# Four graph layers on one core: the attention scores of the edges looked up with a stationary table, edge scores made beside a dense layer, and fewer rows kept in DRAM

## The reference

```python
def gat_block(x, edge_index, edge_attr, ...):     # 3 heads, edge_attr is (E, 16)
    ...
    alpha = a_src[row2] + a_dst[col2] + a_edge    # per edge and head
    alpha = where(alpha >= 0, alpha, 0.2 * alpha)
    ex = exp(alpha - segment_max(alpha, col2)[col2])
    attn = ex / segment_sum(ex, col2)[col2]
    agg = segment_sum(attn[:, :, None] * xp[row2], col2)
```

## Time and profile before

| | |
|---|---|
| median of 3 runs | 3326.29 us (3325.86 to 3333.78) |
| the profiled execution | 3322.32 us, of which the span is 3320.7 us |
| PE busy | 2399.7 us, 72% of the span |
| DVE busy | 1563.3 us, 47% |
| POOL busy | 1430.9 us, 43% |
| ACT busy | 704.2 us, 21% |
| moved by DMA | 627 MB, 189 GB/s over the span |

### The profile page before, as it was taken

One profiled execution on the slowest core, in us unless ns is written; L12 is line 12 of the kernel. 1 busy time (PEld: TensorE's weight loads), 2 busy tenths in 40 slices (PEclk: granted clock), 3 DMA queues, 4 the chain that ended last, 5 costly groups with the idle time before them and its releaser, 6 DMA issues. The chain is left out here.

```text
span 3320.7 us, 68789 instructions
## 1 busy us (share of the span) xinstructions
PE 2399.7 (72%) x21724; PEld 2076.2 (63%) x21725; DVE 1563.3 (47%) x3763; ACT 704.2 (21%) x1093; POOL 1430.9 (43%) x1498
## 2 busy tenths in 40 slices
PE   1599999989899962999969992666530103999965
PEld 0466666679688841888859882566530103999954
DVE  5476666623311165111133335888879201555567
ACT  0077777726200042000010000000000100000033
POOL 4322222213200012122224446777778777776765
PEclk9899999989899975999989996777775555555577
DMA  4378888942688815888869995999972534655611
GB/s 129 99 226 275 275 279 283 285 146 70 182 284 282 282 46 170 252 248 250 249 196 296 290 292 137 184 186 189 182 170 76 160 106 117 153 142 145 144 37 43
DMA packets 560771, 627.36 MB, mean 189 GB/s; under 512 B 265887, under 2 KB 412524, under 8 KB 560041
## 3 DMA queue, kind: packets, MB, share of 16 engines
q1 hardware_dynamic: 258425, 387.60, 38.1%
q10 hardware_dynamic: 252072, 164.25, 19.6%
q0 software_dynamic: 50208, 74.70, 9.3%
HBM read 484.61 MB, written 142.11 MB: 189 GB/s over the span
## 5 line engine op out<-in xcount | busy, mean ns | idle before, releaser
L896 POOL DMA_INDIRECT rows<-x_rows,src_i x832 | 854.1, 1027 | 279.5 <-issue 236.1
L1570 PE MATMUL ps<-slices,wide 128*128 128x250 f16 x7350 | 829.0, 271 | 41.9 <-DMA slices<-adjacency 36.0
L1570 PEld LDWEIGHTS ps<-slices,wide 128*128 128x128 f16 x7350 | 715.9, 98 | 130.6 <-issue 24.2
L1802 PE MATMUL ps<-slices 128*128 128x75 bf16 x4992 | 248.2, 227 | 160.4 <-DVE slices L2544 160.4
L1802 PEld LDWEIGHTS ps<-slices 128*128 128x128 bf16 x4992 | 241.7, 118 | 166.9 <-issue 166.9
L936 POOL TENSOR_TENSOR ea_one<-ea,ones 128x64 f32<-128x64 f32 x250 | 133.9, 536 | 464.0 <-DMA ea<-in_edge_attr 447.0
L1510 PE MATMUL ps<-weighted,slices 128*128 128x57 f32 x1120 | 253.1, 417 | 69.5 <-DVE weighted L2124 69.5
L1510 PEld LDWEIGHTS ps<-weighted,slices 128*128 128x128 f32 x1120 | 247.1, 333 | 69.8 <-DVE weighted L2124 69.8
L1456 PE MATMUL ps<-rows,weighted 128*32 128x128 f32 x2000 | 274.5, 282 | 15.4 <-DMA ea<-in_edge_attr 13.4
L1510 PE MATMUL ps<-weighted,rows 128*128 128x57 f32 x544 | 130.6, 418 | 194.2 <-DMA rows<-x_rows,src_i 170.8
L1510 PEld LDWEIGHTS ps<-weighted,rows 128*128 128x128 f32 x544 | 123.4, 332 | 197.1 <-issue 171.0
(11 more groups left out here) (356 smaller groups left out, 3421.4 us busy)
## 6 DMA issues: line engine op xcount, KB each, us to landing
slices<-adjacency SPq DMA_DIRECT2D x525, 437.5 KB, 5.5
rows<-in_edge_attr SPq DMA_DIRECT2D x250, 256.0 KB
adjacency<-wide ACTq DMA_DIRECT2D x91, 437.5 KB, 3.1
adjacency<-slices ACTq DMA_DIRECT2D x84, 437.5 KB, 3.1
x_of_edges<-rows SPq DMA_DIRECT2D x140, 256.0 KB
slices<-x_of_edges ACTq DMA_DIRECT2D x140, 256.0 KB
slices<-src_low ACTq DMA_DIRECT2D x52, 512.0 KB
rows<-x_rows,src_i POOLq DMA_INDIRECT x832
```

What stands on the lines that cost most here:

```text
L896: pool.indirect_dma_start(out=packed[i][:, c, :], out_offset=None, in_=table, in_offset=bass.IndirectOffsetOnAxis(ap=rows_of, axis=0)).the ...
L1570: mm = pe.matmul(ps_d[b], high_low[:, part, QS * s + q, :], slices[:, s, PN * q:PN * (q + 1)], start=(s == 0 and q == 0 and part == 0), st ...
L1802: mm = pe.matmul(ps_g[:, s, b, c, 0:HEADS * QH], lowT[:, s, b, h, P * c:P * (c + 1)], tab_b[:, n, h, :, :].rearrange("p h i -> p (h i)"), ...
```

## The change

The lookup is turned round. The table (scaled by a power of two, as two fp16 numbers for each score: 17 high parts x 3 heads x 2 = 102 columns, in three parts of 128 sources) is now the stationary operand, and the comparison matrix moves, 512 edges at a time. The sources' low parts (now source modulo 384) are no longer broadcast by DMA: a 1 x 2048 row is loaded, PE spreads it over 128 partitions with a row of ones, and ACT copies the result out of PSUM. The high parts come as bytes, broadcast by DMA to 102 partitions. DVE picks by one comparison and product, and PE adds the picked rows. The scores go out head by head, ACT issues three small stores for each pass. POOL's wait for `scores_begun` is gone.

The edge scores leave this stage. They are made in the second dense product: SP loads the attributes of 32 edges of each partition for a block (`load_ea`), ahead of the last two slices, and DVE multiplies and reduces them (`edge_scores`) between `mean` and the copy of `yb`.

108 groups are stored in place of 140, and 100 are fresh; `sums` begins with 8 stored groups and then takes stored and fresh ones in turn. Some constants and the list of low and high parts are made by a few more small operations near the start and between the first and the second dense product.

```diff
-    KT = 2
-    QH = 25
+    KT = 3
+    QH = 17
+    HI_DIV = KT * P
+    QR = 2 * HEADS * QH
...
-    FRESH = 68
+    MIXED = NP
+    FRESH = RING * MIXED
     STORED = NG - FRESH
-    MIX = 3 * RING
+    FIRST = 2 * RING
+    MIX = 2 * RING
+    ESC = 32
...
+            def load_ea(c, i):
+                to = rows[:, 1 + i, :, :].rearrange("p c f -> p (c f)")[:, 0:ESC * EF].rearrange("p (j e) -> p j e", e=EF)
+                last = (P - 1) * EPP
+                sp.dma_start(to[0:P - 1, :, :], ea16[0:last, :].rearrange("(p j) e -> p j e", j=EPP)[:, bass.ds(ESC * c, ESC), :]
+                             ).then_inc(es_in[i], 16)
...
+                sp.dma_start(to[P - 1:P, 0:n, :], ea16[bass.ds(at, n), :].unsqueeze(0)).then_inc(es_in[i], 16)
...
                     for s in range(SL):
+                        if k == 1 and s == SL - 2:
+                            if not first:
+                                sp.wait_ge(es_made, 2 * q - 3)
+                            load_ea(q, b)
...
-                if SCORES_LEAD <= g < SCORES_LEAD + PASSES:
-                    pool.wait_ge(scores_begun, g - SCORES_LEAD + 1)
...
+            def store_as(k, s, first=False):
...
+                act.activation(as_o[:, s, :], ps_o[s], ACT.Copy).then_inc(as_copied, 1)
+                act.wait_ge(as_copied, u + 1)
+                for h in range(HEADS):
+                    act.dma_start(as_d[h:h + 1, bass.ds(SB * u, SB)].rearrange("h (j e) -> (h j) e", e=SQ), as_o[4 * h:4 * (h + 1), s, :]
...
+            def next_scores(k, s, first=False, begun=False, last=False):
+                u = 2 * k + s
+                copy_low(u + 2, s, 0)
...
+                    store_as(k - 1 + s, 1 - s, first=begun)
+                copy_low(u + 2, s, 1)
+                if not last:
+                    load_low(u + 4, s)
+                act.wait_ge(picked_ready, 2 * u + 2)
+                load_hi(u + 2, s)
...
+            def score_rows(u, s, b, first):
...
+                for h in range(KT):
+                    for c in range(2):
+                        mm = pe.matmul(ps_g[:, b, SQ * c:SQ * (c + 1)], tab_b[:, h, :, :, :].rearrange("p n h i -> p (n h i)"),
+                                       lowT[:, s, h, SH * b + SQ * c:SH * b + SQ * (c + 1)], start=(h == 0), stop=(h == KT - 1))
...
+            def edge_scores(c, u, i):
+                ea_c = rows[:, 1 + i, :, :].rearrange("p c f -> p (c f)")[:, 0:ESC * EF].rearrange("p (j e) -> p j e", e=EF)
+                v.wait_ge(es_in[i], 32 * (u + 1))
...
+                v.tensor_tensor(es_prod, ea_c.unsqueeze(1).to_broadcast([P, HEADS, ESC, EF]),
+                                we_b[:, :, :].unsqueeze(2).to_broadcast([P, HEADS, ESC, EF]), ALU.mult).then_inc(es_made, 1)
+                v.wait_ge(es_made, 2 * c + 1)
+                v.tensor_reduce(es[:, :, bass.ds(ESC * c, ESC)], es_prod, AX.X, ALU.add).then_inc(es_made, 1)
...
-                    lows(16 * (k + 1 + s), 1 - s)
...
+                    lows(u + 1, 1 - s)
+                v.wait_ge(hi_in[s], 16 * (k + 1))
...
+                    v.scalar_tensor_tensor(picked[:, b, :], hi_b[:, s, SH * b:SH * (b + 1)], seg_i[0:QR, 0:1], ps_g[:, b, :],
+                                           ALU.is_equal, ALU.mult).then_inc(picked_ready, 1)
```

More of the change, by code:

```diff
@@ L774, in body @@
                     sp.dma_start(xb[:, b:b + 1, :, :], tiles_of(rows_of, q)).then_inc(pair_landed[b], 16)
-                pairs(sp, body)
+                if k == 1:
+                    whole = (E - (P - 1) * EPP) // ESC // 2 * 2
+                    for q in range(2):
+                        body(q, 0, q, True)
+                    with sp.Fori(1, whole // 2) as u:
+                        for b in range(2):
+                            body(2 * u + b, u, b, False)
+                    for q in range(whole, NP):
+                        body(q, q // 2, q % 2, False)
+                    sp.wait_ge(es_made, 2 * NP - 3)
+                    load_ea(NP, NP % 2)
+                else:
+                    pairs(sp, body)
             load_rows_twice(d0, t["x"])
@@ new lines, in _ @@
+            for s in range(2):
+                next_scores(0, s, first=True)
+            next_scores(1, 0, begun=True)
+            next_scores(1, 1)
+            with act.Fori(2, NIT // 2 - 2) as k:
+                for s in range(2):
+                    next_scores(k, s)
+            for s in range(2):
+                next_scores(NIT // 2 - 2, s, last=True)
+            store_as(NIT // 2 - 2, 1)
+            for s in range(2):
+                store_as(NIT // 2 - 1, s)
+            for s in range(2):
+                act.wait_ge(as_stored[s], 16 * HEADS * (NIT // 2))
@@ L1810, in _, with score_pass @@
+            def score_pass(k, s, first=False, last=False):
+                u = 2 * k + s
+                score_rows(u, s, 0, first)
+                if not (first and s == 0):
+                    sum_picks(u - 1, 1 - s, 1, first)
+                if not last:
+                    spread_low(k + 1, s, 0)
+                score_rows(u, s, 1, first)
+                sum_picks(u, s, 0, first)
+                if not last:
+                    spread_low(k + 1, s, 1)
             scan_turns(0, *SCANS[0])
+            pe.wait_ge(scan_dve, 3)
@@ L1811, in _ @@
+            for s in range(2):
+                for b in range(2):
+                    spread_low(0, s, b, first=True)
             pe.wait_ge(prep_dve, MAX_DVE + 3)
-            with pe.Fori(0, NIT // 2) as k:
+            for s in range(2):
+                score_pass(0, s, first=True)
+            with pe.Fori(1, NIT // 2 - 1) as k:
                 for s in range(2):
-                    for b in range(2):
-                        score_rows(k, s, b)
+                    score_pass(k, s)
+            for s in range(2):
+                score_pass(NIT // 2 - 1, s, last=True)
@@ L1816, in _ @@
+            sum_picks(NIT - 1, 1, 1, False)
             for k in (1, 2):
@@ L2303, in layer0 @@
                 layer_norm(d0, s, n + 1, rb, yb, d0.done)
[L2305 removed]
+            part = [sums_b[:, n * HEADS * P:(n + 1) * HEADS * P] for n in range(2)]
             def weights_beside(q, s):
```

394 lines of the change are left out of this document (210 added, 184 removed).

## The result

| | before | after |
|---|---|---|
| median of four runs each | 3327.26 us | 3468.69 us (3464.78 to 3469.28) |
| ratio to before, 95% interval | 1 | 1.0426 (1.0408 to 1.0443) |
| span of the profiled execution | 3320.7 us | 3463.2 us |

The kernel became 4.3% slower. The stages of after, as in the earlier trace rows: length, busy PE, PEld, DVE, ACT, POOL, then PEclk, DMA share, GB/s. The first is the whole second dense product, the second a piece of the score stage, the third a piece of `sums`.

What follows compares the result with a forecast made beforehand. It took PE to bound the second dense product and POOL's gathers with PE's sums the last third; 3322.3 + 211 - 25 = 3508 us, hence 3512 because the median lies 4 us above the profiled run; range 3420 to 3610.

Steps and rivals of the forecast that it cites:

- The dense product: Second dense product: the 127-row load on one DMA engine sets a block's period, 22.6 us for 14.16, +211 us.
- the bounds: Second dense product: one DMA engine's rate lies between 18.9 and 28 GB/s, giving +304 to +91 us.
- Rival B: Second dense product: the 127 rows spread over many engines, or that engine has room; only -25 us left, 3301 us; chance 0.08.
- the signs I had named: Second dense product: 560 to 580 us, PE under 70% busy awaiting slices, under 245 GB/s, blocks of 20 to 26 us.
- D: Second dense product: PE idles some 8 us per block and runs the rest at 1.2 GHz; +354, 3655 us; chance 0.06.
- DVE's operations, the lists, the constants: Dense product and before: two DVE operations, 1.75 us each, hidden; lists and constants nothing, or 4 and 3 us.
- The score stage: Score stage: a pass takes 6 to 6.5 us for 7.9, the stage 70 to 90 us shorter, ACT slowest.
- C: Score stage: the pass runs at 1.2 GHz, 8.7 us, scores end late and POOL waits; 3550 us; chance 0.10.
- The gathers: Gathers and `sums`: POOL no longer waits for PE, -20.6 us, and less stretching under the scores; together -25 us.
- -4: Score stage: stretching of gathers under the score passes belongs to fewer gathers, -4 us.

Runs made afterwards that it cites:

- e2_five: The changed kernel with the 127-row attribute load cut into 125 and 2 rows: 3296.21 us, 0.9934 of the kernel before on its chip.
- e2_two: The changed kernel with the 127-row attribute load cut into 122 and 5 rows: 3353.02 us, 1.0044 of the kernel before on its chip.
- e5_one_cmp: The changed kernel with its load cut into 112 and 15 rows, without two of DVE's three comparisons from the third score pass on: 3266.83 us, ratio 0.9849.
- e4_mix: The kernel before with only the new order of groups (108 stored, 100 fresh): 3288.25 us, 0.9904 of the kernel before on its chip.

## Why the prediction was right, and where it was off

**The dense product.** The step held: 127 rows went to one engine, its work was the period, PE's 14.16 us hid behind it. The size was off by the rate, 22 GB/s from the two-engine tail; the engine worked at 23.9, so 20.88 us for 22.6, and +168 for +211. That is the miss of 43 us (3512 for 3469). The 18.9 and 28 of the bounds held it. Rival B's point of decision, 311 kB at 22 GB/s, four engines, agrees with e2_five, hidden with 291 kB, and e2_two, not hidden with 365.

Of the signs I had named, the waits for slices, the 20 to 26 us of a block and the lower GB/s (177) came. The stage was shorter than I had said (529 us for 560 to 580), by the same rate, and PE was busy 78% of it and not under 70%: at the lower clock it was busy 411 us for the work that had taken 353 (see D).

**DVE's operations, the lists, the constants.** 1.75 us each as said, hidden. The dense product started 2.6 us earlier than before, so nothing is seen of a cost of what stands ahead of it; the runs e2_five and e5_one_cmp, alike up to there, start it 7 us apart (1321.4 and 1314.4), so a few us could not be told.

**The score stage.** I took 6 to 6.5 us for a pass with ACT as its slowest queue. It took 5.55 us (L2684 from 2509.24 to 2514.78), and ACT was busy 44% of 2240 to 2500 us. The stage took 296 us (2233.3 to 2529.0), 110 less than before, where I had said about 320. DVE waits for ACT's copy:

```profile
2509.24 2.09 DVE L2684 TENSOR_SCALAR slices<-wide,slot_p 128x2048 f16<-128x2048 f16 x3 [1.09 <-ACT wide L1306]
...
2514.78 2.09 DVE L2684 TENSOR_SCALAR slices<-wide,slot_p 128x2048 f16<-128x2048 f16 x3 [1.09 <-ACT wide L1306]
```

Between them stand the picks of 2.45 us for both halves, so DVE is busy 4.5 of the 5.55 us, and PE is busy 91% of the stretch. It is a circle of the three: in each pass PE waits for DVE's pick (44 waits of L1878 in 2240 to 2500 us), ACT waits for PE to spread the low parts (L1889, 153.7 us in all), and DVE waits for ACT's copy. Naming ACT was wrong, and it cost nothing, since the stage is ahead of need: POOL never waited for PE there. PE's 20 matmuls were busy 5.1 us to a pass where I had 4.3. The clock was 0.98, so C did not come.

**The gathers.** The predicted -25 and the measured -26 (-12 and -14) agree by luck. POOL's waits for PE went, as said: of its 127.3 us idle in `sums` 418 x 0.304 = 127.1 are the usual gap. The mixture did that, as e4_mix shows. But "under the scores it belongs to fewer gathers: -4" was wrong: the stretching belongs to the passes, of which there are still 52, and each has three comparisons for two. It grew from 23 us to 220 x 0.154 = 34 us, and e5_one_cmp shows that the comparisons make it. Against that stood a gain that I had not looked for, 11 of the 14 us behind the last gather.

**D.** PE stood idle (529 - 411) / 25 = 4.7 us in each block, where I had some 8, and the granted clock of the stage was 0.88 on average: a matmul of L1632 took 297 ns where it takes 270 at the full clock. Behind the mean stand both levels. After a wait of 5.45 us, PE begins at 1460.76 us (windows):

```profile
1460.00:1464.00 4.00, 3.24 (x16) 2.49 (x17) 0.00 (x0) 0.00 (x0) 0.59 (x1) 0.50 0.95 322
1464.00:1468.00 4.00, 4.00 (x27) 3.08 (x26) 0.53 (x2) 0.38 (x1) 2.43 (x3) 0.65 0.42 130
1468.00:1472.00 4.00, 4.00 (x32) 3.54 (x30) 3.79 (x3) 0.68 (x2) 0.00 (x0) 1.00 0.26 52
```

The clock was at 0.50 and back at 1.00 within the block. The Trainium skill holds that idle gaps between bursts of matmuls send the clock back to its lower level (TensorE: Matmul & The Clock Gate, section "HAM oscillation — how this bites in real kernels"); these rows agree. What D had wrong is that PE would run the rest of the block at 1.2 GHz. What PE lost by the clock lay behind the transfers.

## What to carry to other kernels

Before a transfer is called small, look at how many DMA engines its rows can be dealt to: a load that adds 8% to the bytes of its stage cost 5% of the kernel with 127 rows and nothing with 112 + 15, 125 + 2, or from POOL's queue. For an engine whose gaps are full, ask what its neighbour's operations do to each of its instructions, per pass and not per us. A reordering that uses the slack of a stage should be tried where that stage is slow: the mixture alone gave -1.0% and +3.3% on two chips. The change with its load split gave 0.9896 and 0.9934, and on the slow chip 0.9863 with a slower form of the comparisons; there POOL waited 13.9 us for the sums, and 164.5 with the mixture alone. With the fast comparisons it was not run on that chip.

## What was not expected of the hardware

- An issue is not free when the engine behind it is full: the DMA behind a 127-row load took SP 10.1 to 12.2 us and ACT 14.7 to 17.8 us to issue, and 0.23 us behind 112 + 15 rows.
- DVE operations lengthen POOL's indirect gathers by their operands: 0.94 us beside picks with one operand in PSUM, 1.42 beside fp16 comparisons in SBUF, 1.96 to 3.99 beside an operation with two arrays in SBUF, up to 1.55 beside the scans, and 0.94 beside a reciprocal with one input in SBUF. The Trainium skill has this (SBUF — State Buffer, section "Who interferes with whom"): GpSimd shares ports with DVE, the fast modes of tensor_scalar block it, and a DVE instruction with two inputs in SBUF contends with a GpSimd instruction that reads SBUF. The times agree with both (1.42 and 1.96 to 3.99 us); the ports themselves no trace shows. The prediction took the stretch from a mean over the stage, and missed what it hangs on.
